# Adjacency tiles turned by DMA instead of by TensorE, with steps of the nearest-neighbour search moved to other places

## What is computed

```python
def _knn_indices(xyz, k):
    sq = jnp.sum(xyz * xyz, axis=1)
    d2 = sq[:, :, None] + sq[:, None, :] - 2.0 * jnp.einsum('bdn,bdm->bnm', xyz, xyz)
    _, idx = jax.lax.top_k(-d2, k)
    return idx
...
idx_t = jnp.transpose(idx, (0, 2, 1))[:, None, :, :]
for i in range(NUM_BLOCKS):                      # 4
    shortcut = points
    p = _lrelu(points)
    g = _group_point(p, idx_t)
    c = jnp.einsum('oi,bin->bon', w_center[i], p)
    gn = jnp.einsum('oi,bikn->bokn', w_neighbor[i], g)
    points = (c + gn.sum(axis=2)) / (K + 1.0) + shortcut
...
idx = _knn(x_loc, 30)
rel = pts[bidx, idx] - pts[:, :, None, :]
...
att = jax.nn.softmax(h[..., 0], axis=-1)
xk = x.transpose(0, 2, 1)[bidx, idx]
agg = jnp.einsum('bnkc,bnk->bnc', xk, att)
return x + agg.transpose(0, 2, 1)
```

## Time and profile before

| | us |
|---|---|
| median of 3 runs | 706.3 (705.44 to 706.35) |
| the profiled execution, its own time | 706.24 |
| its span in the profile | 704.5 |
| PE busy | 685.8 (97%) |
| DVE busy | 580.3 (82%) |
| ACT busy | 349.2 (50%) |
| POOL busy | 327.3 (46%) |

### The profile page before, as it was taken

One profiled execution on the slowest core, in us unless ns is written; L12 is line 12 of the kernel. 1 busy time (PEld: TensorE's weight loads), 2 busy tenths in 40 slices (PEclk: granted clock), 3 DMA queues, 4 the chain that ended last, 5 costly groups with the idle time before them and its releaser, 6 DMA issues.

```text
span 704.5 us, 13228 instructions
## 1 busy us (share of the span) xinstructions
PE 685.8 (97%) x5478; PEld 580.2 (82%) x5478; DVE 580.3 (82%) x854; ACT 349.2 (50%) x531; POOL 327.3 (46%) x264
## 2 busy tenths in 40 slices
PE   6999999999999999999999999999999999999998
PEld 4799889878888888788888987987987877888887
DVE  5699999999799899966789898886896998678831
ACT  6456547348526227866794354383473443233210
POOL 2268767665806527500039667667779850000000
PEclk9999999999999999999999999999999999999999
DMA  9610300210000012744442722613524740101001
GB/s 351 189 3 1 119 1 8 84 30 1 1 1 0 2 63 87 251 146 170 170 147 76 119 75 77 103 63 103 89 86 125 109 74 1 47 32 45 32 33 59
DMA packets 32140, 55.86 MB, mean 79 GB/s; under 512 B 11344, under 2 KB 11600, under 8 KB 32080
## 3 DMA queue, kind: packets, MB, share of 16 engines
q1 hardware_dynamic: 26304, 43.48, 18.0%
q0 software_dynamic: 5248, 10.49, 9.1%
q10 hardware_dynamic: 528, 1.05, 0.4%
HBM read 40.98 MB, written 12.71 MB: 76 GB/s over the span
## 4 chain that ended last, share of the span: by engine, by line
PE 71%; DVE 12%; POOL 7%; issue 4%; ACT 4%; DMA 1%; SPq 0%; POOLq 0%; ACTq 0%
PE bank L1595 22%; PE bank L1619 5%; PE bank L1657 5%; PE bank L1621 5%; PE bank L1620 5%; PE bank L1719 4%; PE bank L1760 4%; PE bank L1762 4%; PE bank L1505 4%; PE bank L1761 4%; PE bank L1507 4%; PE bank L1506 4%; POOL p_second L558 3%; POOL pts_l L569 3%; DVE idx L1085 2%
## 5 line engine op out<-in xcount | busy, mean ns | idle before, releaser
L1595 PE MATMUL bank<-nbr,pts_h 128*128 128x512 f32 (+2 forms) x512 | 193.3, 380 | 3.1 <-POOL pts_l L569 1.6
L1595 PE MATMUL bank<-nbr,pts_l 128*128 128x512 f32 (+2 forms) x512 | 190.4, 374 | 0.0
L558 POOL TENSOR_TENSOR p_second<-p_first,p_second 128x512 f32<-128x512 f32 x58 | 77.0, 1332 | 124.6 <-ACT p_second L815 124.6
L1595 PEld LDWEIGHTS bank<-nbr,pts_h 128*128 128x128 f32 x512 | 96.8, 189 | 20.8 <-POOL pts_l L569 3.4
L1595 PEld LDWEIGHTS bank<-nbr,pts_l 128*128 128x128 f32 x512 | 96.9, 189 | 14.9 <-issue 0.2
L829 ACT CAST pts_h<-bank 128x512 fp32r<-128x512 f32 (+2 forms) x64 | 34.9, 554 | 144.0 <-PE bank L1595 140.9
L1619 PE MATMUL bank<-wT,pts_h 128*128 128x512 f32 x256 | 102.1, 399 | 0.3 <-DVE pts_l L1119 0.3
L1621 PE MATMUL bank<-wT,pts_l 128*128 128x512 f32 x256 | 99.9, 390 | 0.0
L1620 PE MATMUL bank<-wT,pts_h 128*128 128x512 f32 x256 | 99.8, 390 | 0.0
L569 POOL TENSOR_TENSOR pts_l<-p_second,pts_h 128x512 fp32r<-128x512 f32 x58 | 79.6, 1378 | 2.8 <-ACT pts_h L821 2.0
L1505 PE MATMUL bank<-pts_h 128*128 128x512 f32 (+3 forms) x192 | 69.2, 361 | 7.8 <-DVE pts_l L1045 7.3
(11 more groups left out here) (220 smaller groups left out, 1429.5 us busy)
## 6 DMA issues: line engine op xcount, KB each, us to landing
p_rows<-p_second SPq DMA_DIRECT2D x32, 256.0 KB, 2.0
more<-a_rows SPq DMA_DIRECT2D x17, 480.0 KB, 4.3
scratch<-a_rows SPq DMA_DIRECT2D x15, 480.0 KB, 4.5
X<-in_ctx SPq DMA_DIRECT2D x12, 512.0 KB, 6.1
out_dram<-X SPq DMA_DIRECT2D x15, 256.0 KB, 2.0
more<-in_ctx SPq DMA_DIRECT2D x4, 512.0 KB, 5.6
X<-in_x SPq DMA_DIRECT2D x2, 1024.0 KB, 5.3
X<-in_x SPq DMA_DIRECT2D x1, 1536.0 KB, 6.9
```

The costliest lines, as they stand in the source:

```text
L558: pool.tensor_tensor(p, a, b, ALU.subtract).then_inc(s_p32, 1)
L1595: mm = pe.matmul(bank[u % 3][:, 0:w], p[:, m, t * P:(t + 1) * P], nbr[b][:, m, hf * HALF:hf * HALF + w], start=(m == 0 and part_ == 0), st ...
```

## The change

All 128 transposes of `adj_turn` leave PE. SP issues one DMA transpose per tile instead, SBUF to SBUF, into a landing buffer; `nbr_out` copies from there and no longer from PSUM. Tiles 0 to 6 land in the two halves of the columns of `nbr0` that belong to tile 7, which is written last (`nbr_out` of tile 7 therefore waits for the copy of tile 6); tiles 7 to 15 land in two buffers in `scratch`. On SP's queue turns 0 and 1 stand ahead of X's first loads, 2 to 5 ahead of the 1536 KB load, 6 to 9 between it and the last load of X, 10 to 15 behind. A turn waits for the diagonal of its tile and for `nbr_out` two tiles before; tile 7 also for the norms of batch 1 on PE.

Adjacency places 3, 6 and 9 become 4, 7 and 10 (14 stays); `nbr_out` stays two places behind its adjacency. The extras of the search change from 4 steps at place 0 and 1 at place 1 to 2 and 1, 1 at place 15 and 4 at place 16. The index rows move two places forward, and as the search ends at place 41 instead of 43, G0 falls from 44 to 42.

```diff
+        def landing(T):
+            if T < NT - 1:
+                c0 = (NT - 1) * P + T % 2 * P // 2
+                return nbr0_land[:].bitcast(BF16)[:, :, 2 * c0:2 * c0 + P]
+            o = (SC + 1) * N + T % 2 * HALF
+            return scratch[:, o:o + HALF].bitcast(BF16).rearrange("p (m n) -> p m n", m=NT)
...
-            n = STEPS_AT[g % 16] + {0: 4, 1: 1}.get(g, 0)
+            n = STEPS_AT[g % 16] + {0: 2, 1: 1, 15: 1, 16: 4}.get(g, 0)
...
-        ADJ_AT = {3: (8, 9), 6: (10, 11), 9: (12, 13), 14: (14, 15)}
+        ADJ_AT = {4: (8, 9), 7: (10, 11), 10: (12, 13), 14: (14, 15)}
...
-        ROWS_AT = {30: 0, 33: 1, 36: 2, 44: 3}
+        ROWS_AT = {28: 0, 31: 1, 34: 2, 42: 3}
...
+            def adj_turn(T):
+                sp.wait_ge(s_diag, T + 1)
+                if T == NT - 1:
+                    sp.wait_ge(s_sqmm, 2 * NH)
+                if T >= 2:
+                    sp.wait_ge(s_nbr, T - 1)
+                sp.dma_start_transpose(landing(T), adj[:, T % 2, :]).then_inc(s_adjT[T % 2], 16)
+
+            adj_turn(0)
+            adj_turn(1)
             for i, (t0, t1) in enumerate(((0, 4), (4, 8))):
...
             for i, (t0, t1) in enumerate(((0, 6), (6, 8))):
 
+                for T in (range(6, 10) if i else range(2, 6)):
+                    adj_turn(T)
                 sp.wait_ge(s_p1, AHEAD)
...
-            sp.wait_ge(s_adjT, TILES)
+            for T in range(NT + 2, TILES):
+                adj_turn(T)
+            sp.wait_ge(s_nbr, TILES)
...
             def nbr_out(T):
-                act.wait_ge(s_adjT, T + 1)
+                act.wait_ge(s_adjT[T % 2], 16 * (T // 2 + 1))
+                if T == NT - 1:
+                    act.wait_ge(s_nbr, T)
                 if T == NT:
                     act.wait_ge(s_sel, NT)
                 act.copy(nbr[T // NT][:, :, (T % NT) * P:(T % NT + 1) * P],
-                         bank[6 + T % 2][:].bitcast(BF16).rearrange("p (m n) -> p m n", m=NT)) \
-                    .then_inc(s_nbr, 1)
+                         landing(T)).then_inc(s_nbr, 1)
...
                 if T >= 2:
-                    act.wait_ge(s_adjT, T - 1)
+                    act.wait_ge(s_adjT[T % 2], 16 * (T // 2))
...
-            def adj_turn(T):
-                pe.wait_ge(s_diag, T + 1)
-                if T >= 2:
-                    pe.wait_ge(s_nbr, T - 1)
-                for m in range(NT):
-                    mm = pe.transpose(bank[6 + T % 2][:].bitcast(BF16)[:, m * P:(m + 1) * P],
-                                      adj[:, T % 2, m * P:(m + 1) * P], ident_b[:])
-                mm.then_inc(s_adjT, 1)
```

More of the change, by code:

```diff
@@ L76, in build @@
         pts_l = sb("pts_l", [P, KT, N], F32R)
+        with nc.sbuf_tensor("nbr0_land", [P, NT, N], F32) as nbr0_land:
+            pass
         nbr0 = sb("nbr0", [P, NT, N], F32R)
@@ L255, in build @@
         s_diag = sem("adj_diagonal_ready")
-        s_adjT = sem("adj_transposed")
+        s_adjT = [sem(f"adj_transposed{i}") for i in range(2)]
         s_nbr = sem("nbr_ready")
@@ L1555, in _ @@
             gram(3)
-            adj_turn(0)
             gram(4)
             gram(5)
-            adj_turn(1)
             gram(6)
@@ L1562, in _ @@
             gram(8)
-            adj_turn(2)
-            adj_turn(3)
             gram(9)
             gram(10)
-            adj_turn(4)
             gram(11)
-            adj_turn(5)
             gram(12)
@@ L1573, in _ @@
             gram(15)
-            adj_turn(6)
             norms(1)
@@ L1668, in side @@
             def side(g):
[L1669 to L1672, removed]
                 if g in TURN_AT:
```

## The result

| | before | changed |
|---|---|---|
| median | 707.49 us (703.90 to 709.21, 14 runs) | 709.88 us (708.74 to 710.92, 14 runs) |
| span of the profiled execution | 704.5 us | 708.4 us |

The ratio is 1.0047, 95% interval 1.0034 to 1.0060: slower by 2.4 to 4.2 us. The forecast was 700.9 us.

A forecast was written before the change was run, and what follows sets the result against it. PE, busy 97%, was taken as the bound, with DVE full before 187 us; 4.2 us kept plus 1.2 at the lookups gave 5.4 off 706.24, forecast 700.9 us; own range 699.0 to 702.5, all rivals 698.0 to 706.0.

The forecast's parts named there:

- Score phase: Before pass 0: seven turns leave PE, 3.2 us, so pass 0 starts about 3.1 us earlier, near 126.2.
- Pass 0, head of pass 1: Aggregate 4 starts at 143.0 after `q_low(1)`; pass 1 starts at 179.9; then POOL's `p_low` and DVE's `q_low(8)` end late.
- the 1 to 3 us given: Sign at the head of pass 1: PE waits 1 to 3 us for `p_low`.
- the 4.2 us kept at pass 2: Start of pass 2: 233.5 instead of 237.7, so 4.2 us kept of some 8.8.
- The lookups: Pass 2: first lookup near 274.3, its stall on DVE's one-hot leaves; pass ends at 292, another 1.4 us, taken as 1.2.
- The turn: Score phase: a DMA turn taken at 4.5 us; tiles 10 and 11 wait 0.6 us, tile 6 lands near 131.
- rivals 2 and 3: Turn by DMA slow, kernel slower than before (chance 0.14); turn takes 6 to 7 us, 702.3 to 704.5 (chance 0.14).
- ACT idle over 2 us for the DMA: Sign against the forecast: it is wrong if ACT idles over 2 us waiting for the DMA turns.
- The rest, at nothing: Lookups, network and spreads are the same work two places earlier, covered by busy PE; `nbr_out` from SBUF also costs nothing.
- passes 4 to 7 not as long as before: Sign against the forecast: it is wrong if passes 4 to 7 change in length.
- Rival 4: Passes 4 to 6: ACT's moved network work falls among `p_halves`; 3 to 5 us come back, 704 to 706; chance 0.13.
- the sum: Whole kernel: 4.2 + 1.2 = 5.4 us gained, from 706.24 to 700.8; stated as 700.9 us.

The follow-up runs named there:

- search_table_alone: Kernel before, turns still on PE, with the change's search steps, adjacency places and index rows, G0 kept at 44: 703.68 us, ratio 0.9945.
- g0_44: Changed kernel with G0 put back from 42 to 44, so lookups, network and spreads stand where they did before: 700.05 us, ratio 0.9913.
- g0_43: Changed kernel with G0 = 43, so lookups, network, attention parts and spreads are one place earlier than before, not two: 700.76 us, ratio 0.9923.
- the one more step: Changed kernel with only the lookups early, and one more search step moved from place 0 to place 16 of the extras: 698.95 us, ratio 0.9894.
- network_only_early: Changed kernel with lookups and network two places early, but index columns, attention parts and spreads at the places of before: 702.13 us, ratio 0.9926.
- first_onehot_early: Changed kernel with the first one-hots of the spreads made at place 112, ahead of pass 7's first q_low: 706.70 us, ratio 1.0010.
- spreads_later: Changed kernel with the spreads alone two places later, at place 115 as before: 705.01 us, ratio 0.9987.
- search_table_g0_42: Kernel before, turns still on PE, with the change's search table and G0 = 42: 713.42 us, ratio 1.0086.
- dma_turns_alone: Changed kernel with the search extras and index rows of before, so G0 is 44; adjacency places stay changed: 702.39 us, ratio 0.9951.

## Why the prediction was wrong

**Score phase, right in kind, 0.5 too much.** Forecast gain 3.1 us. The kernels of one table show 129.4 with turns on PE (search_table_alone) and 126.8 without (g0_44): 2.6. I had said that POOL's last norm work moves with ACT's copies; PE now waits 0.5 us for it, just ahead of pass 0. The changed kernel's profiled execution began another 0.4 us late, in the loads of ctx.

**Pass 0, head of pass 1, right.** `q_low(1)` ends last at aggregate 4, as argued: forecast 143.0, the row 143.75, g0_44 143.4. POOL's last `p_low` was forecast at 188.9, and VectorE's `q_low(8)` at 192.1 (answers to the earlier trace rows):

```profile
186.12 2.52 POOL L593 TENSOR_TENSOR pts_l<-p_second,pts_h 128x512 fp32r<-128x512 f32 x2
```

```profile
191.74 0.69 DVE L1138 TENSOR_TENSOR pts_l<-bank,pts_h 128x512 fp32r<-128x512 f32 x1
```

They ended at 188.6 and 192.4. The wait for `p_low` was in the 1 to 3 us given, 1.26. Of the 4.2 us kept at pass 2, 3.6 are there, 3.8 in g0_44.

**The lookups, right, with a slip.** The first lookup was forecast at 274.3 and came at 275.0. The end of pass 2 at 292 was a wrong addition: five pairs and four `wp` from 274.3 end near 297, and 297.8 was measured. Against before that is equal, but with two pairs (4.5 us) more done. The gain to there was 4.5, and 4.7 at pass 4; the forecast 5.4.

**The turn, right in the median.** 3.2 us where 4.5 was taken, rivals 2 and 3 out, tile 6 landed at 127.6 (by 131 forecast). I had looked only at tile 6 behind its load of X; tiles 2 and 3 stand behind one too, and ACT waited 2.8 us there. That is one of the signs that the prediction named against itself (ACT idle over 2 us for the DMA), and it came without a cost. That I took the slower value for all turns cost nothing either, as ACT had slack. `nbr_out` takes 1.05 us from SBUF and took 1.02 before: put at nothing, rightly.

**"The rest, at nothing": the step that failed.** I wrote that lookups, network and spreads are the same work two places earlier, with PE as cover. The cover was asked of the wrong engine: PE was covered, but VectorE's fixed order was not. Three pieces of its work changed what they stand beside: four network steps more (4.8 us) ahead of `q_low`(4, 0), the attention parts beside POOL's p chain, the first one-hots inside the interleaved pair. They were worth 9.5 us and not 0, against a gain of 6.2. The new order, though not its price, was to be seen without a run: the orders of VectorE up to place 77 and from 110 to 115 show them, and I looked only at those of passes 0 and 1. The sign that the prediction named for this, passes 4 to 7 not as long as before, came: pass 4 took 50.4 us and not 48.5, pass 7 72.9 and not 63.9.

**Rival 4** had the right side and the wrong place. It gave 3 to 5 us, 704 to 706, to ACT's network work falling among `p_halves`. `p_low` did come late at one head, but beside VectorE's attention parts: PE waits 1.5 us for it there, 0.8 in g0_44. The largest part, 4.2 us by the ratios, is in the one-hots behind the pair and the half clock that follows. With G0 held at 44 the gain is 6.2 us where the sum has 5.4. Its interval, 4.9 to 7.4, holds the sum.

## What to carry to other kernels

When the places of a later stage count from the end of an earlier one, shortening the earlier stage moves everything behind it, and that move is a change of its own: hold the offset (here one constant) and measure the two apart. Same work two places earlier is free only where each in-order engine keeps the same neighbours, so compare the order on every engine at each pairing of stages, and look for a small operation that PE waits for and that stands behind a wait of its own engine. If it must move, the better pick here was to move the lookups alone: 699.2 and 699.9 us in two measurements, 0.9 to 1.2% below the kernel before; g0_44, g0_43 and the one more step aren't told apart from it.

## What the runs showed of the hardware

- A DMA transpose of 128 x 1024 bf16 within SBUF landed in 3.0 to 3.5 us in 12 cases of 16 (changed kernel); the three issued right after loads of 1 or 1.5 MB on the same queue took 5.4 to 7.8. SP needed 1.24 to 1.37 us in the median to issue one and 3.38 at most. In the changed kernel's trace neither VectorE nor PE idles behind one.
- VectorE and POOL slow each other on elementwise work in SBUF: 1.22 to 2.28 us on one side, 1.29 to 1.99 on the other, at the same time.
- The clock granted to PE fell to its 1.2 GHz level after an idle of 3.58 us that followed two shorter ones. Of the waits in pass 4 it fell after those of 2.34 and 2.37 us (network_only_early, first_onehot_early) and not after 2.21, 2.25 and 2.31 (spreads_later, changed, search_table_g0_42); but in dma_turns_alone it fell shortly after waits of 2.03 us (pass 0; granted clock 0.64 from 140 to 144 us) and 1.33 us (first lookup; 0.57 from 284 to 288), and in the kernel before not after the same 1.33. So the length of the one idle doesn't tell it.
- It also fell between 304 and 320 us, behind the narrow matmuls of the lookups and with PE hardly idle, in 11 of the 13 profiles of this case.
- What followed a stall was of its own order: 2.6 us of work lost behind 3.58 us idle, 1.6 to 1.7 behind 2.34 and 2.37. A comparison within 2 us has to look at the clock row first.
